# Loads from two queues and layer-norm moments combined for all tiles at once, in the opening stage of a four-block kernel

## The reference

```python
x = x + _L0_attn_ref(_layernorm(x, axis=-1), ...)   # 16 heads, causal softmax attention
x = x + _L0_ffn_ref(_layernorm(x, axis=-1), ...)    # 16 experts, 4 chosen for each token, and a shared one
x = x + _L1_attn_ref(_layernorm(x, axis=-1), ...)   # 16 heads, attention by hyperbolic distance
x = x + _L1_ffn_ref(_layernorm(x, axis=-1), ...)    # relu MLP

def _layernorm(x, axis=-1, eps=1e-05):
    m = jnp.mean(x, axis=axis, keepdims=True)
    v = jnp.var(x, axis=axis, keepdims=True)
    return (x - m) / jnp.sqrt(v + eps)
```

## Time and profile before

| | us |
|---|---|
| median of 3 runs (lowest, highest) | 2552.72 (2552.12, 2556.64) |
| the profiled execution, its own time | 2551.49 |
| the profiled execution, its span (first to last instruction) | 2549.7 |
| busy PE, DVE, ACT, POOL | 2143.9, 1992.2, 1857.0, 1644.3 |
| start of the first attention stage's first instruction on ACT | 47.17 |

### The profile page before, as it was taken

The page is one execution under the profiler, slowest core; times in us unless marked ns, Lnnn a source line. Parts: engine busy times, 40 slices in busy tenths (PEclk is TensorE's granted clock), DMA queues, the critical chain, the costliest instruction groups (busy, mean ns, idle before and its releaser), DMA issues. The chain is left out here.

```text
span 2549.7 us, 48293 instructions
## 1 busy us (share of the span) xinstructions
PE 2143.9 (84%) x14935; PEld 1539.4 (60%) x14935; DVE 1992.2 (78%) x6007; ACT 1857.0 (73%) x3188; POOL 1644.3 (64%) x1387
## 2 busy tenths in 40 slices
PE   4999999999999979999957777777777777776599
PEld 4777777777777758888844444444444444443276
DVE  4677777777777747787768999999999999999522
ACT  2666666666666634444239999999999999999743
POOL 2766766676667500000049999999999999999500
PEclk7999999999999969999967777787777877777599
DMA  5000000000000024435300000000000000000011
GB/s 137 1 2 2 1 1 0 1 0 1 1 0 1 2 67 102 101 70 123 77 1 1 1 1 1 1 1 1 1 1 1 1 1 1 1 1 1 9 29 37
DMA packets 44132, 49.86 MB, mean 20 GB/s; under 512 B 5112, under 2 KB 27038, under 8 KB 43934
## 3 DMA queue, kind: packets, MB, share of 16 engines
q1 hardware_dynamic: 35614, 43.32, 7.0%
q10 hardware_dynamic: 8320, 4.19, 0.7%
HBM read 42.78 MB, written 4.72 MB: 19 GB/s over the span
## 5 line engine op out<-in xcount | busy, mean ns | idle before, releaser
L1459 POOL TENSOR_TENSOR u<-u,spare 128x1024 f32<-128x1024 f32 x256 | 597.2, 2377 | 38.1 <-ACT spare L1432 38.1
L545 ACT ACTIVATE prob<-s_ps,nmax 128x128 f32<-128x128 f32 (+1 forms) x1024 | 364.9, 432 | 139.8 <-DVE nmax L602 139.8
L602 DVE CUSTOM_DVE_ANT_0 s_ps<-s_ps,mask 128x128 f32<-128x128 f32 (+1 forms) x1024 | 341.3, 385 | 101.8 <-issue 78.0
L1526 DVE TENSOR_SCALAR u<-d_ps 128x1024 f32<-128x1024 f32 x256 | 311.6, 1217 | 49.8 <-PE d_ps L1352 49.5
L582 POOL TENSOR_TENSOR g_lo<-g_all,g_hi 128x512 fp32r<-128x512 f32 x256 | 329.0, 1285 | 21.3
L1531 DVE SCALAR_TENSOR_TENSOR u<-i_ps,u 128x1024 f32<-128x1024 f32 x256 | 313.5, 1225 | 14.0 <-DVE u L1526 0.4
L1469 POOL TENSOR_TENSOR spare<-spare,u 128x1024 f32<-128x1024 f32 x128 | 303.1, 2368 | 10.7
L1446 ACT ACTIVATE u<-u 128x1024 f32<-128x1024 f32 x256 | 257.3, 1061 | 0.3
L1449 ACT ACTIVATE u<-u 128x1024 f32<-128x1024 f32 x256 | 256.4, 1056 | 0.0
L1352 PE MATMUL d_ps<-rowsT 28*128 28x256 f32 x1024 | 150.9, 374 | 121.8 <-DVE u L1526 118.9
L1352 PE MATMUL i_ps<-rowsT 6*128 6x256 f32 x1024 | 159.4, 397 | 107.1 <-DVE u L1531 106.6
(11 more groups left out here) (263 smaller groups left out, 5446.0 us busy)
## 6 DMA issues: line engine op xcount, KB each, us to landing
w_all<-w_rows SPq DMA_DIRECT2D x128, 256.0 KB, 5.6
x<-L_attn_x ACTq DMA_DIRECT2D x8, 512.0 KB, 13.7
y<-y_rows SPq DMA_DIRECT2D x16, 256.0 KB, 2.3
wkqv<-L_attn_Wkqv SPq DMA_DIRECT2D x4, 528.0 KB, 8.6
gate_rows<-L_ffn_gate_proj SPq DMA_DIRECT2D x1, 512.0 KB, 14.4
up_rows<-L_ffn_up_proj SPq DMA_DIRECT2D x1, 512.0 KB, 11.6
down_cols<-L_ffn_down_proj SPq DMA_DIRECT2D x1, 512.0 KB, 13.1
w_rows<-wT SPq DMA_DIRECT2D x8, 64.0 KB, 1.6
```

Of the source, the lines that this page charges most:

```text
L545: last = nc.scalar.activation(prob[:, kind, at, :].rearrange("p c n -> p (c n)"), s_ps[kind][:, at.start * P:at.stop * P], ACT.Exp, bias=n ...
L602: last = nc.vector.tensor_tensor_reduce(out=scores, in0=scores, in1=keep.mask[:, N - width:N], scale=-1.0, scalar=3.4e38, op0=ALU.add, op1 ...
L1459: nc.gpsimd.tensor_tensor(u[:, slot(i, p), :], u[:, slot(i, p), :], spare[:, p % SPARE, :], ALU.add).then_inc(sum_done, 1)
L1526: nc.vector.tensor_scalar(u[:, slot(i, p), :], d_ps[:, :], 0.0, None, ALU.max).then_inc(dist_done, 1)
```

## The change

Four of the eight transfers of x (tiles 32 to 63) go from ACT's queue to SP's, behind the weights `wkqv` and ahead of the gate weights. DVE does the `bn_stats` of all 64 tiles in one row, ahead of its copies of `wv`, `biases` and `b1T`. The 64 `bn_aggr` are replaced by seven instructions over all tiles at once: with the two halves' means and sums of squared deviations, the mean is half the sum of the means, and the variance is (sum of both squared deviations + 32 x (difference of means)^2) / 128. ACT's square root waits for the last of the seven.

```diff
@@ sync
                 for g in range(1, H // 4):
                     sp.dma_start(wkqv[:, 4 * g:4 * g + 4, :], w[:, 4 * g:4 * g + 4, :]).then_inc(wkqv_in[g], 16)
+                x = io["L0_attn_x"].rearrange("b (j p) d -> p (b j) d", p=P)
+                for t in range(tiles // 2, tiles, 4 * TB):
+                    sp.dma_start(keep.x[:, t:t + 4 * TB, :], x[:, t:t + 4 * TB, :]).then_inc(x_in[1], 16)
                 sp.dma_start(gate_rows[:, :, :],
@@ scalar
-                for t in range(0, tiles, 4 * TB):
-                    act.dma_start(keep.x[:, t:t + 4 * TB, :], x[:, t:t + 4 * TB, :]).then_inc(x_in[2 * t // tiles], 16)
+                for t in range(0, tiles // 2, 4 * TB):
+                    act.dma_start(keep.x[:, t:t + 4 * TB, :], x[:, t:t + 4 * TB, :]).then_inc(x_in[0], 16)
                 nc.scalar.preload_act_table_set("sqrt_and_others")
...
-                act.wait_ge(var_done, tiles)
+                act.wait_ge(combined, 7)
@@ vector
-                def aggregates(some):
-                    dve.wait_ge(stats_done, some[-1] + 1)
-                    for t in some:
-                        v.bn_aggr(keep.mv[:, t, :], keep.stats[:, t, :]).then_inc(var_done, 1)
+                def combine():
+                    halves = lambda n: keep.stats[:, :, n]
+                    sum_mean, gap, sum_m2 = (total[:, n, :] for n in range(3))
+                    dve.wait_ge(stats_done, tiles)
+                    v.tensor_tensor(sum_mean, halves(1), halves(4), ALU.add).then_inc(combined, 1)
+                    v.tensor_tensor(gap, halves(1), halves(4), ALU.subtract).then_inc(combined, 1)
+                    v.tensor_tensor(sum_m2, halves(2), halves(5), ALU.add).then_inc(combined, 1)
+                    dve.wait_ge(combined, 3)
+                    v.tensor_scalar(keep.mv[:, :, 0], sum_mean, 0.5, None, ALU.mult).then_inc(combined, 1)
+                    v.scalar_tensor_tensor(out=gap, in0=gap, scalar=P / 4.0, in1=gap, op0=ALU.mult, op1=ALU.mult
+                                           ).then_inc(combined, 1)
+                    dve.wait_ge(combined, 5)
+                    v.tensor_tensor(sum_m2, sum_m2, gap, ALU.add).then_inc(combined, 1)
+                    dve.wait_ge(combined, 6)
+                    v.tensor_scalar(keep.mv[:, :, 1], sum_m2, 1.0 / P, None, ALU.mult).then_inc(combined, 1)
...
                     if n == turned:
                         stats(range(0, tiles // 2))
-                    if n == turned + H // 4 + 3:
                         stats(range(tiles // 2, tiles))
-                        aggregates(range(0, tiles // 2))
-                        aggregates(range(tiles // 2, tiles))
+                        combine()
```

More of the change, by code:

```diff
@@ L110, in load_and_fold @@
         x_in = [m.sem(f"x_in{half}") for half in range(2)]
+        total = m.sb("moments_total", [P, 3, tiles])
+        combined = m.sem("combined0")
         ones_set, rounded = m.sem("ones_set"), m.sem("rounded")
@@ L113, in load_and_fold @@
         eps_set = m.sem("eps_set")
-        stats_done, var_done, std_done, inverted = m.sem("stats_done0"), m.sem("var_done0"), m.sem("std_done0"), m.sem("inverted0")
+        stats_done, std_done, inverted = m.sem("stats_done0"), m.sem("std_done0"), m.sem("inverted0")
         bank_full, read_by_dve, read_by_act = m.sem("bank_full"), m.sem("read_by_dve"), m.sem("read_by_act")
```

## The result

| | before | changed |
|---|---|---|
| median of 19 runs, us | 2552.12 | 2561.5 |
| lowest, highest, us | 2546.11, 2569.24 | 2551.11, 2568.57 |
| span of the profiled execution | 2549.7 | 2549.3 |
| ratio of the changed kernel to before | | 1.0033, 95% interval 1.0021 to 1.0044 |

The change made the kernel slower by 0.33%, against a forecast of 0.31% faster. The profiled execution is the fastest of the changed kernel's runs and hides most of that.

The account below looks back on a forecast made before the run. The opening stage was taken as a DVE chain with one hole: 4.84 (hole) + 0.17 (small wait) + 2.8 (moments) gave 7.8 us, so 2552.72 - 7.8 = 2544.9 us, range 2541.5 to 2549.5.

Parts of the forecast that it names:

- The end of the opening stage: DVE's chain before the attention stage: first subtraction at 34.9 us instead of 42.69, a gain of 7.8 us.
- The hole: DVE's idle time ahead of 31.44 in the opening stage, 4.84 us, claimed to go with all statistics in one row.
- the seven instructions: DVE's replacement of the 64 bn_aggr: 1.4 us instead of 4.21, a gain of 2.8; bounds 0.5 and 4.1.
- jobs 21 to 25: PE's jobs around DVE's first subtractions: up to 1 us late at the low clock, nothing at the high clock.
- The lone queue: SP's queue, alone after 17.4 us, moves 551 packets per us: x lands at 24.9, the last load at 33.1.
- Rival 2: A lone SP queue moves only its shared rate, so loads bound the opening stage: 4.4 us slower, 2557.1; chance 0.05.
- ACT's freed queue at nothing: Fewer issues on ACT let PE's folds start near 21.2 instead of 24.44, counted as no gain in the sum.
- Everything behind the barrier moves with it: All stages after the opening were claimed to start earlier by its whole gain, 7.8 us, otherwise unchanged.
- Rival 1: Attention stage starts earlier but its clock rises no earlier: 3.9 us given back, time 2548.8; chance 0.12.
- the rise after the opening: Rise of the granted clock in the attention stage, expected at about 63 us; staying near 70 would contradict the prediction.
- slower by over 0.2%: Outcome class for the whole kernel, given 0.04: half of rival 2 and half of the unassigned remainder.

Follow-up runs that it names:

- e5: The changed kernel run again unaltered, on another chip: median 2557.51 us, 1.0035 of the kernel before.
- e6: The changed kernel with eight satisfied waits (4 instructions) added on ACT, second measurement, on another chip: median 2541.28 us, 0.996 of the kernel before.
- e1: The changed kernel with eight satisfied waits (4 instructions) added on ACT, first measurement: median 2568.23 us, 0.9959 of the kernel before on that chip.
- e4: The changed kernel with all eight transfers of x back on ACT's queue: median 2572.11 us, 0.9962 of the kernel before on that chip.
- e10: The changed kernel with 2 more instructions (4 satisfied waits) on ACT: profiled execution 2541.82 us.
- e12: The changed kernel with 128 more instructions (256 satisfied waits) on ACT: profiled execution 2568.36 us.
- e8: The changed kernel with 4 more instructions on ACT and 64 more on PE: median 2552.2 us, 0.9998 of the kernel before.

## Why the prediction was wrong

- **The end of the opening stage: right.** The hole went (4.84), the seven instructions took 1.40 (forecast 1.4), the first subtraction came at 34.50 (34.9), and jobs 21 to 25 cost about 0.7 through the low clock, within the 1 us that was named. The attention stage opened at 39.68 (39.4). That the seven took just 1.4 is in part luck: the first three took 0.67 (33.15 - 32.48) where the sum had 0.53, with starts 0.19 apart and not 0.13. The prediction reads its source on overlap incompletely: the same paragraph of the Trainium skill, "VectorE: DVE Perf Modes", section "The DRAIN you can't avoid", adds that a next instruction which is not held starts earlier. The three, 0.27 us each, do so.
- **The lone queue: right.** There is no gap in the row of 64 statistics, so the second half of x was there in time. `wp`, the last transfer, was issued at 32.08 and landed 2.0 later, at 34.1 (33.1). Job 24 did not wait for it: it came at 36.35, straight behind PE's own nine transposes, as the prediction had it for the low clock. What was late were the gate and up rows, at which PE waited 0.83 and 2.48, all within DVE's cover. Rival 2 did not occur.
- **ACT's freed queue at nothing: right for the opening stage.** The folds started at 20.96, and DVE, busy with the statistics, had no use for them until 33.88. This was the item that decided everything, though: I counted time for each issue that goes, and not that each is an instruction whose absence moves all code behind it.
- **The step that failed** is "Everything behind the barrier moves with it, since the later stages share no transfer or state with this one." They share the place of their code. Measured in its place: 12.0 us more in the attention stage from the two traces, and 16.2 between the medians of e5 and e6. The clock that falls behind the gaps can make up the difference (in the profiled execution of e5 it cost 7 us), but the executions behind the medians have no traces.
- **Rival 1** looked for the give-back at the right kind of place (the clock behind a gap) but at the wrong one: the rise after the opening came at 62.8, and the clock fell at the loop's branches in e5 instead. None of my rivals had the mechanism, and slower by over 0.2% had been given 0.04.
- What could have shown it beforehand: the trace of before has no pause of ACT or PE at the branch, but DVE's row above, five waits of up to 2.4 us that no semaphore ends, was there to be read, as were the pairs of 52.1 us across the branch against 51.5 inside the body. That the stage has such a loop, and that the edit changes the length of three engines' programs ahead of it, stood in the code.

Open: why PE's pause occurs in most executions on one chip and less often on two others, with the same program. This is read from the traces (of e1 to e4 against e5, e6 and e10 to e12) and from the times of the kernel before, which was not traced on those chips. e8 shows that the place of its loop decides how likely it is, not what decides within one place.

## What to carry to other kernels

An edit that removes or adds instructions in front of a hardware loop moves the loop's start, and in a long loop that can cost more than the edit gains; look at the first instructions behind each branch back, for a wait that no semaphore ends, and at the count of instruction packets, before judging the edit. Such a wait on any engine of the kernel before is a warning, even where it costs nothing yet. To measure what an edit is worth, compare both kernels with the loop written out, or restore the place with a few instructions that do nothing. A gap of 3 us on PE has more than one price, since the clock may fall behind it: expect a spread and take several runs.

## What the hardware showed that was not expected

- With more packets on the instruction queue, a branch back of ACT took 2.4 to 2.9 us to the first instruction and, at two of the places, 2.1 to 2.5 more to the next, against 0.2 and 0.4 otherwise. Four instructions, of 689 that ACT runs up to the first of these branches in the kernel before, switch it on or off.
- DVE, with a loop of 574 instructions, paused 2.7 to 3.7 us at every pass of every kernel with the loop. In its loop of 37 instructions in the last stage the next instruction came 0.1 to 0.3 us behind the branch.
- On PE the like took 3.4 to 5.1 us, with nine more packets a pass on queue 8, each of 16 KB (88 of them carry 1.44 MB in the kernel before), where those of queue 14 are 8 KB.
- The kernel before was near 2552 in most runs on two chips and near 2576 in most on a third.
